# A mixture-of-experts token pass: gate logits with tokens on partitions, expert coefficients spread by a 0/1 product

## The chip, the cores and the metric

The kernel runs on one core of a Trainium2 chip (trn2). The metric is the device time of one execution in microseconds; lower is better. A core has TensorE (PE), VectorE (DVE), ScalarE (ACT), GpSimd (POOL) and SyncE (SP), which here starts all DMAs. The engines run side by side and wait for each other by semaphores.

## What is computed

The input x has 4 x 1024 tokens of 128 numbers. Three layers follow each other, each on the layer-normalised input: x + 0.5 ffn, x + attention (16 heads, ALiBi, rotary), x + 0.5 ffn. Both ffn layers use the same weights. Cut to what matters:

```python
scores = sigmoid(xf @ gate.T)                      # N x 8 experts
sfc = scores + corr_bias
# of 2 groups of 4 experts keep the one whose two best sfc sum higher
sel = top_k(where(mask, sfc, 0.0), 2)
top = scores[sel] / (scores[sel].sum(-1) + 1e-20)  # two coefficients per token
lat = xf @ fc1_w.T
routed = sum over the two experts e of top_e * (relu2(lat @ w1[e].T) @ w2[e].T) @ fc2_w.T
shared = relu2(xf @ up_w.T) @ down_w.T             # relu2(a) = max(a, 0) ** 2
return routed + shared
```

## The kernel before

The program is a prologue (weights are loaded, turned and folded), `token_pass` number 1 (ffn, then q, k and v of the attention), a bound for the softmax, the attention, and `token_pass` number 2 (output projection of the attention, then ffn). The change lies in the prologue and in `token_pass`, which is built twice.

**Chunks.** A pass goes over eight chunks of 512 tokens, four tiles of 128 (`in_chunks`: lead, body for each chunk, tail). Every engine has its own list of steps in `body`, written out by hand; an engine does its steps in that order, and this order sets what stands behind what. PE's body, for chunk c: in pass 2 the projection of the next chunk; hidden 0 to 3 (the shared experts' 512 hidden features), hidden 4, then spread 0 to 3 with hidden 5 to 7 (the 8 x 64 routed features) between them; `turn` of the next chunk's normalised input after spread 0 and `gate` of the next chunk after spread 2 (L682 to L689); `turn_gate` of the next chunk; `outputs`. In pass 1 the q, k and v products of the chunk before come between the first tile of `outputs` and the other three.

**Precision.** x_t, the turned input, is kept as two fp32r parts, high (copied by ACT, L719) and low (high subtracted from it by DVE, L953), and each weight matrix as w_hi and w_lo. A product of the two is three products (`times_weights`, L557). A plain fp32 product, as in `outputs`, shows as two matmuls in the trace; a transpose or an fp32r product as one.

**Gate.** `gate` (L586) multiplies w[:, 0:128], of whose columns 8 are the gate and 120 are zero, as stationary operand with the 512 tokens: the logits come out with experts on partitions. ACT copies the 128 x 512 result to `logit_t` (L725), PE turns it by four transposes (`turn_gate`, L591), and ACT takes exp of 8 columns in each tile (L731). DVE's `route` (L985 to L1045) makes the two coefficients per token from that: some 20 small operations, `coef` being the last (L1043).

**Coefficients.** The routed hidden features lie with features on partitions and tokens in the row, so each coefficient has to stand on 64 partitions. ACT's `widen` repeats each of the 8 coefficients 64 times in the row, [128 tokens, 4 tiles, 512] (L740), behind everything else in its body, so right in front of the next chunk's relu 0. `spread_coef` m then turns four 128 x 128 blocks of it into a PSUM bank (L608), and DVE's `scale` m multiplies the squared features by that (L1053). Two banks are used in turn.

**The other engines.** ACT: relu of each hidden block (L751), the square of the routed ones (L758). POOL: the squares of the shared ones (L843), rstd by a power (L835); in pass 2 the rstd of the next chunk stands in front of the squares. DVE, in pass 1: scale 0 to 3 with the second layer norm of the chunk before between them (L924) and `take_low` after scale 1; moments (L902); rotary products (L1075); `route` of the next chunk; centre; `rotary_q`; `residual` (L1061). In pass 2: `merge` (L944), moments, centre (L924), scale 0 to 3 with `take_low` after scale 1, `normalise_o` (L933, L934), `route`, `residual`. SP: in the prologue all loads one behind the other (`fold_loads`, `loads`, `table_loads`, x, rope), in the passes the loads and stores of a chunk.

**Prologue.** DVE waits for all of `table_loads` (L348) and then does, in order, the casts and copies of the tables, the parts of the slopes, and w_all, w_out and w_lo, which end the prologue.

## Time and profile before

| | before |
|---|---|
| device time, median of 3 runs | 1017.91 us (1016.92 to 1019.26) |
| profiled execution, its own time | 1016.92 us |
| its span in the profile | 1016.9 us |
| PE matmul busy | 866.5 us (85%) |
| DVE busy | 605.9 us (60%) |
| ACT busy | 699.4 us (69%) |
| POOL busy | 151.0 us (15%) |
| pass 1, first to last instruction, about | 27 to 282 us |
| pass 2, about | 827 to 1017 us |

The times in the profile are microseconds from the start of the span. L557 is line 557 of the kernel. PE is the matmuls, PEld the weight loads, which overlap them; matmuls are pipelined, so the time from one start to the next says what one costs, and its duration says when its result is there. A group "x4" is four instructions in a row, and its duration runs from the start of the first to the end of the last. In brackets stands how long the engine had been idle in front of the instruction, and what it waited for. In names like p_ps_g the number of the pass is left out.

### The profile page before, as it was taken

How to read it: one execution, taken by the hardware profiler on the slowest of the kernel's cores; microseconds unless marked ns; L12 is line 12 of the kernel's file. 1: busy time of each engine (PE TensorE's matmuls, PEld its weight loads, DVE VectorE, ACT ScalarE, POOL GpSimd, SP SyncE). 2: the span in 40 equal slices, each digit the busy share in tenths (PEclk: the TensorE clock that was granted, in tenths of full speed). 3: DMA queues.
4: the chain of work that ended last, by engine and by line, in shares of the span. 5: the costliest groups of instructions: out<-in, count | busy, mean ns of one | idle time of the engine just before them, and what ended most of it. 6: DMA issues, size and time to landing. Idle time of an engine off the chain costs nothing. (4 is left out here: it accounts for less than half of the span.)

```text
span 1016.9 us, 17952 instructions
## 1 busy us (share of the span) xinstructions
PE 866.5 (85%) x5629; PEld 432.3 (43%) x5629; DVE 605.9 (60%) x1620; ACT 699.4 (69%) x890; POOL 151.0 (15%) x136
## 2 busy tenths in 40 slices
PE   3498888788608999999999999999999947887888
PEld 2376666666502222222222222222222216776777
DVE  3469888888634454555445544555445437777673
ACT  1264343444417999999999999999999924555453
POOL 5224343334310000000000000000000001123211
PEclk9999999998758999999999999999999977999999
DMA  5112022211153322343223432344223021122100
GB/s 170 31 32 74 29 60 73 65 61 54 54 104 63 46 42 41 51 59 43 40 42 53 59 41 39 43 54 59 41 38 47 15 70 34 42 64 62 41 11 22
DMA packets 55095, 52.58 MB, mean 52 GB/s; under 512 B 7405, under 2 KB 42677, under 8 KB 54849
## 3 DMA queue, kind: packets, MB, share of 16 engines
q1 hardware_dynamic: 55052, 52.06, 26.2%
q8 instruction: 21, 0.34, 0.1%
q14 instruction: 22, 0.18, 0.1%
HBM read 36.15 MB, written 15.86 MB: 51 GB/s over the span
## 5 line engine op out<-in xcount | busy, mean ns | idle before, releaser
L1624 ACT ACTIVATE at_weights<-at_scores 128x1024 f32<-128x1024 f32 x512 | 495.4, 1022 | 31.2 <-DVE at_scores L1593 27.0
L1593 DVE SCALAR_TENSOR_TENSOR at_scores<-diag,at_now,at_scores 128x128 f32<-128x128 f32 x512 | 181.2, 354 | 234.8 <-PE at_scores L1530 217.8
L1530 PE MATMUL at_scores<-q_op,k_op 75*128 75x512 bf16 (+7 forms) x1408 | 273.0, 325 | 26.4 <-POOL at_start L1508 19.2
L1545 PE MATMUL at_acc<-at_weights,at_v_op 128*9 128x512 f32 x2048 | 267.5, 595 | 0.5 <-ACT at_weights L1624 0.5
L1530 PEld LDWEIGHTS at_scores<-q_op,k_op 75*128 75x128 bf16 (+1 forms) x1408 | 109.4, 98 | 312.4 <-issue 179.0
L623 PE MATMUL p_ps_o<-w_out,p_hid 128*128 128x128 f32 x1024 | 120.2, 278 | 0.4 <-DVE p_hid L1053 0.4
L557 PE MATMUL p_ps_h<-p_xn_t,w_hi 128*128 128x512 f32 x256 | 96.5, 461 | 27.1 <-ACT p_relu L751 26.5
L623 PEld LDWEIGHTS p_ps_o<-w_out,p_hid 128*128 128x128 f32 x1024 | 117.8, 194 | 0.6 <-DVE p_hid L1053 0.6
L751 ACT ACTIVATE p_relu<-p_ps_h 128x512 f32<-128x512 f32 x128 | 74.8, 591 | 35.3 <-PE p_ps_h L557 33.2
L713 ACT ACTIVATE p_coef_wide<-p_coef 128x512 f32<-128x512 f32 x64 | 35.0, 617 | 78.2 <-DVE p_coef L1043 78.2
L868 POOL MEMSET p_minus_half<- 128x4 f32 x2 | 0.2, 104 | 518.5 <-POOLq L1433 518.5
L843 POOL TENSOR_TENSOR p_hid<-p_relu 128x512 f32<-128x512 f32 x64 | 64.7, 1041 | 26.3 <-ACT p_relu L751 26.3
L557 PEld LDWEIGHTS p_ps_h<-p_xn_t,w_hi 128*128 128x128 f32 x256 | 46.2, 211 | 49.0 <-ACT p_relu L751 42.9
L1545 PEld LDWEIGHTS at_acc<-at_weights,at_v_op 128*9 128x9 f32 x2048 | 30.4, 88 | 79.5 <-issue 68.1
L557 PE MATMUL p_ps_h<-p_xn_t,w_lo 128*128 128x512 f32 x128 | 55.3, 432 | 0.0
L835 POOL TENSOR_TENSOR p_rstd<-p_veps,p_minus_half 128x4 f32<-128x4 f32 x24 | 24.3, 1012 | 190.6 <-DVE p_veps L917 190.6
L713 ACT ACTIVATE p_v_ext<-p_ps_q 128x128 f32<-128x128 f32 x32 | 6.3, 283 | 57.3 <-PE p_ps_q L651 57.3
L578 PE MATMUL p_ps_t<-ident,p_xn 128*128 128x128 f32 x64 | 10.9, 298 | 36.6 <-DVE p_xn L924 36.6
L758 ACT ACTIVATE p_squared<-p_relu 128x512 f32<-128x512 f32 x64 | 40.4, 632 | 2.0
L713 ACT ACTIVATE p_xn_t<-p_ps_t 128x512 fp32r<-128x512 f32 x24 | 14.2, 592 | 38.8 <-PE p_ps_t L578 35.4
L1053 DVE TENSOR_TENSOR p_hid<-p_squared,p_ps_q 128x512 f32<-128x512 f32 x32 | 21.9, 684 | 23.7 <-PE p_ps_q L608 22.4
L924 DVE TENSOR_SCALAR p_xn<-p_x,p_mean,p_rstd 128x128 f32<-128x128 f32 x32 | 28.9, 964 | 9.6 <-POOL p_rstd L835 9.6
(165 smaller groups left out, 808.0 us busy)
## 6 DMA issues: line engine op xcount, KB each, us to landing
q_op<-q_parts SPq DMA_DIRECT2D x144, 64.0 KB
k_op<-k_parts SPq DMA_DIRECT2D x144, 64.0 KB
q_parts<-p_parts SPq DMA_DIRECT2D x8, 384.0 KB, 2.6
k_parts<-p_parts SPq DMA_DIRECT2D x8, 384.0 KB, 3.3
v_scratch<-p_v_ext SPq DMA_DIRECT2D x32, 72.0 KB, 1.6
at_v_op<-v_scratch SPq DMA_DIRECT2D x16, 144.0 KB, 13.1
o_scratch<-at_o_out SPq DMA_DIRECT2D x64, 36.0 KB
x_ln<-in_L_attn_x_dram SPq DMA_DIRECT2D x8, 256.0 KB, 3.7
```

What stands on the lines that cost most here:

```text
L557: last = nc.tensor.matmul(out, w[:, col:col + P], x_t[:, part, :], start=(i == 0), stop=(i == 2))
L623: last = nc.tensor.matmul(ps_o[:, t, :], hid[:, m, t * P:(t + 1) * P], w_out[:, m, :], start=(m == 0), stop=(m == HT - 1))
L713: return nc.scalar.activation(dst, src, ACT.Copy)
L751: nc.scalar.activation(relu[:, m, :], ps_h[:, m % 2, :], ACT.Relu).then_inc(relu_ready, 1)
L758: nc.scalar.activation(squared[:, m, :], relu[:, ST + m, :], ACT.Square).then_inc(sq_act, 1)
L835: nc.gpsimd.tensor_tensor(rstd[:, which, :], veps[:, which, :], minus_half[:, :], ALU.pow).then_inc(rstd_ready[which], 1)
L843: nc.gpsimd.tensor_tensor(hid[:, m, :], relu[:, m, :], relu[:, m, :], ALU.mult).then_inc(sq_pool, 1)
L924: return v.tensor_scalar(dst[:, t, :], src[:, t, :], mean[:, which, t:t + 1], rstd[:, which, t:t + 1], ALU.subtract, ALU.mult)
L1530: last = nc.tensor.matmul(scores[:, u % SLOTS, lo:hi], k_op[par][0:rows, j, kt * P:(kt + 1) * P], q_op[par][0:rows, j, lo:hi], start=True, ...
L1545: last = nc.tensor.matmul(acc[32 * j:32 * j + VW, cols], v_op[par][:, kt, VW * j:VW * (j + 1)], weights[:, kt % PSTEPS, j, cols], start=(k ...
L1593: v.scalar_tensor_tensor(out=block_at, in0=diag[:, 0, :], scalar=now[:, par, j, 0:1], in1=block_at, op0=ALU.mult, op1=ALU.add).then_inc(di ...
L1624: nc.scalar.activation(weights[:, kt % PSTEPS, j, :], scores[:, u % SLOTS, :], ACT.Exp).then_inc(slots_free, 1)
```

## The change

The gate's product is turned round: x_t is the stationary operand (12 loads of 128 x 128: four tiles, three terms), the 8 gate columns of w_hi and w_lo are the moving one, and the logits come out with tokens on partitions, [128, 4 x 8], in one bank. `take_logits` and `turn_gate` go (4 transposes and one ACT copy), and with them `logit_t`. `widen` goes too (4 ACT operations).

DVE's `route` ends with three operations instead of one: the coefficients rounded to fp32r, the exact ones, and the difference of the two, so that `coef_parts` holds 16 columns a tile. PE turns them in `turn_coef` (four transposes of 128 x 16), between hidden 3 and hidden 4 of the same chunk, ACT copies the [16, 512] result to `coef_t` in `take_coef`, between relu 3 and relu 4. `spread_coef` is then one fp32r product: `spread_rows` (16 x 128 of a 0/1 matrix that says which expert a feature belongs to, high and low rows both) with coef_t, in place of four transposes. The prologue loads that 0/1 matrix (16 x 512, on SP's queue behind `headsum_f32`) and DVE copies it to fp32r. The first chunk's `turn_gate` and `widen` in the leads go as well.

```diff
@@ prologue
                 (headsum_f32[:, :], consts["headsum"]),
+                (spread_f32[:, :], consts["spread"]),
                 (bias_f32[br, :, :], consts["biasrows"]),
...
                 v.tensor_copy(headsum[:, :], headsum_f32[:, :])
+                v.tensor_copy(spread_rows[:, :], spread_f32[:, :])
@@ PE
                 if c.at_least >= 1:
-                    pe.wait_ge(gate_exp, c.n)
-                times_weights(ps_g[:, :], 0, xn_t[:, c.half]).then_inc(gate_made, 1)
-
-            def turn_gate(c):
-                pe.wait_ge(gate_copied, c.n + 1)
+                    pe.wait_ge(coef_copied, c.n)
+                x_t = xn_t[:, c.half]
                 for t in range(TILES):
-                    last = nc.tensor.transpose(ps_g[:, t * P:(t + 1) * P], logit_t[:, t * P:(t + 1) * P],
+                    for i, (part, w) in enumerate(((0, w_hi), (1, w_hi), (0, w_lo))):
+                        last = nc.tensor.matmul(ps_g[:, EXPERTS * t:EXPERTS * (t + 1)], x_t[:, part, t * P:(t + 1) * P],
+                                                w[:, 0:EXPERTS], start=(i == 0), stop=(i == 2))
+                last.then_inc(gate_made, 1)
+
+            def turn_coef(c):
+
+                pe.wait_ge(coef_ready, c.n + 1)
+                for t in range(TILES):
+                    last = nc.tensor.transpose(ps_g[0:2 * EXPERTS, t * P:(t + 1) * P], coef_parts[:, t, :].bitcast(F32),
                                                ident[:, :])
-                last.then_inc(gate_turned, 1)
+                last.then_inc(coef_turned, 1)
...
-                for t in range(TILES):
-                    last = nc.tensor.transpose(wide_bank[m % 2][:, t * P:(t + 1) * P],
-                                               coef_wide[:, t, m * P:(m + 1) * P], ident[:, :])
-                last.then_inc(spread, 1)
+                nc.tensor.matmul(wide_bank[m % 2], spread_rows[:, m * P:(m + 1) * P], coef_t[:, :],
+                                 start=True, stop=True).then_inc(spread, 1)
...
+                turn_coef(c)
                 hidden(c, ST)
-                pe.wait_ge(wide_ready, c.n + 1)
+                pe.wait_ge(coef_copied, c.n + 1)
...
-                if not end:
-                    turn_gate(c.next())
-
                 outputs(c, [0])
@@ ACT
-            def widen(c):
-
-                act.wait_ge(coef_ready, c.n + 1)
+            def take_coef(c):
+
+                act.wait_ge(coef_turned, c.n + 1)
                 if c.at_least >= 1:
                     act.wait_ge(spread, RT * c.n)
-                for t in range(TILES):
-                    last = copy(coef_wide[:, t, :].rearrange("p (e i) -> p e i", i=INTER),
-                                coef[:, t, :].unsqueeze(2).broadcast_to([P, EXPERTS, INTER]))
-                last.then_inc(wide_ready, 1)
+                copy(coef_t[:, :], ps_g[0:2 * EXPERTS, :]).then_inc(coef_copied, 1)
@@ DVE, end of route
-                v.tensor_tensor(coef[:, :, :], chosen[:, :, :],
-                                crec[:, :].unsqueeze(2).broadcast_to([P, TILES, EXPERTS]),
-                                ALU.mult).then_inc(coef_ready, 1)
+                each = crec[:, :].unsqueeze(2).broadcast_to([P, TILES, EXPERTS])
+                v.tensor_tensor(coef_parts[:, :, 0:EXPERTS], chosen[:, :, :], each, ALU.mult)
+                v.tensor_tensor(coef[:, :, :], chosen[:, :, :], each, ALU.mult).then_inc(route_step, 1)
+                dve.wait_ge(route_step, r + 16)
+                v.tensor_tensor(coef_parts[:, :, EXPERTS:2 * EXPERTS], coef[:, :, :], coef_parts[:, :, 0:EXPERTS],
+                                ALU.subtract).then_inc(coef_ready, 1)
```

## Rows read from the trace of the kernel before

**Rows 1.** Three stretches: busy PE, PEld, DVE, ACT, POOL (instructions); clock, DMA share, GB/s

```profile
65.00:240.00 175.00, 142.64 (x875) 113.92 (x874) 151.60 (x386) 78.11 (x161) 70.36 (x59) 0.97 0.20 59
857.00:998.00 141.00, 121.56 (x819) 102.95 (x818) 102.69 (x288) 68.53 (x123) 30.05 (x30) 0.98 0.14 40
898.00:901.00 3.00, 3.00 (x11) 2.30 (x10) 1.07 (x2) 1.67 (x3) 0.00 (x0) 0.50 0.02 5
```

**Rows 2.** Waits of DVE in pass 1, 65 to 240 us: total, times, longest

```profile
DVE p_turn_a L1075 <- PE p_ps_q L557: 9.3, 12, 1.7
DVE p_hid L1053 <- PE p_ps_q L608: 4.3, 6, 0.7
DVE p_hid L1053 <- ACT p_squared L758: 3.3, 1, 3.3
```

**Rows 3.** Timeline of one period of pass 2: start, duration, PE and DVE

```profile
875.72 0.66 PE L578 MATMUL p_ps_t<-ident,p_xn 128*128 128x128 f32 x4 [2.61 <-DVE p_xn L924]
...
877.65 0.69 DVE L1053 TENSOR_TENSOR p_hid<-p_squared,p_ps_q 128x512 f32<-128x512 f32 x1 [1.39 <-PE p_ps_q L608]
...
879.00 0.73 PE L557 MATMUL p_ps_g<-p_xn_t,w_hi 128*128 128x512 f32 x2 [0.35 <-DVE p_xn_t L953]
...
879.56 0.39 PE L557 MATMUL p_ps_g<-p_xn_t,w_lo 128*128 128x512 f32 x1
...
879.79 0.60 PE L608 MATMUL p_ps_q<-ident,p_coef_wide 128*128 128x128 f32 x4
...
881.14 7.31 PE L623 MATMUL p_ps_o<-w_out,p_hid 128*128 128x128 f32 x64
...
882.34 0.17 DVE L989 TENSOR_SCALAR p_en<-p_en 128x32 f32<-128x32 f32 x1
...
887.31 0.19 DVE L1043 TENSOR_TENSOR p_coef<-p_chosen,p_crec 128x32 f32<-128x32 f32 x1
...
888.28 1.06 PE L566 MATMUL p_ps_q<-proj_t,p_o_norm 128*128 128x128 f32 x8
...
888.48 0.69 DVE L1061 SCALAR_TENSOR_TENSOR p_res<-p_ps_o,p_x 128x512 f32<-128x512 f32 x1 [0.98 <-PE p_ps_o L623]
...
889.43 0.69 DVE L944 TENSOR_TENSOR p_x<-p_x_biased,p_ps_q 128x512 f32<-128x512 f32 x1 [0.26 <-PE p_ps_q L566]
...
897.15 0.66 PE L578 MATMUL p_ps_t<-ident,p_xn 128*128 128x128 f32 x4 [2.50 <-DVE p_xn L924]
...
903.62 1.61 PE L623 MATMUL p_ps_o<-w_out,p_hid 128*128 128x128 f32 x13
```

**Rows 4.** Timeline of v's product in pass 1: weight loads

```profile
170.19 0.30 PEld L651 LDWEIGHTS p_ps_q<-w_hi,p_xn_t 128*128 128x128 f32 x2 [0.52 <-DVE p_turn_a L1075]
...
170.41 0.19 PEld L651 LDWEIGHTS p_ps_q<-w_lo,p_xn_t 128*128 128x128 f32 x1
...
171.53 5.44 PEld L623 LDWEIGHTS p_ps_o<-w_out,p_hid 128*128 128x128 f32 x48
```

**Rows 5.** Timeline, waits in three other chunks (1 and 7; 0 of pass 2)

```profile
66.53 0.73 PE L557 MATMUL p_ps_h<-p_xn_t,w_hi 128*128 128x512 f32 x2 [0.85 <-ACT p_relu L751]
...
244.61 0.69 DVE L1053 TENSOR_TENSOR p_hid<-p_squared,p_ps_c 128x512 f32<-128x512 f32 x1 [0.65 <-ACT p_squared L758]
...
854.67 0.69 DVE L1053 TENSOR_TENSOR p_hid<-p_squared,p_ps_c 128x512 f32<-128x512 f32 x1 [0.75 <-ACT p_squared L758]
```

**Rows 6.** Timeline, first chunk of pass 1

```profile
42.86 0.19 DVE L1043 TENSOR_TENSOR p_coef<-p_chosen,p_crec 128x32 f32<-128x32 f32 x1
...
43.09 2.18 ACT L713 ACTIVATE p_coef_wide<-p_coef 128x512 f32<-128x512 f32 x4 [5.23 <-DVE p_coef L1043]
...
51.94 0.69 DVE L1053 TENSOR_TENSOR p_hid<-p_squared,p_ps_c 128x512 f32<-128x512 f32 x1 [8.88 <-PE p_ps_c L608]
```

**Rows 7.** Line 1021 in the whole span: duration in ns, least/median/most

```profile
L1021 DVE TENSOR_TENSOR p_above<-p_kept x16: 424/426/1365, 39.8 to 992.8; 128x256 f32<-128x256 f32 x16
```

**Rows 8.** Timeline of the prologue, DVE's wait for the tables

```profile
18.94 1.22 DVE L349 CAST bias_rows<-bias_f 30x2048 bf16<-30x2048 f32 x1 [6.22 <-DMA bias_sel<-const_biassel]
```

More of the change, by code:

```diff
@@ L64 @@
 UNITS = KT * GH
-ROUTE_STEPS = 15
+ROUTE_STEPS = 16
 QKV_COL = P
@@ L133, in shape_constants @@
     c["ident"] = np.eye(P, dtype=np.float32)
+    row, wide = np.arange(2 * EXPERTS)[:, None], np.arange(EXPERTS * INTER)[None, :]
+    c["spread"] = (row % EXPERTS == wide // INTER).astype(np.float32)
     c["headsum"] = (np.arange(P)[:, None] // HD == np.arange(HEADS)[None, :]).astype(np.float32)
@@ L442, in token_pass @@
         coef = sb("coef", [P, TILES, EXPERTS])
-        coef_wide = sb("coef_wide", [P, TILES, EXPERTS * INTER])
+        coef_parts = sb("coef_parts", [P, TILES, 2 * EXPERTS], F32R)
+        coef_t = sb("coef_t", [2 * EXPERTS, CHUNK], F32R)
         relu = sb("relu", [P, HT, CHUNK])
@@ L670, in lead @@
                 gate(Chunk(0, 0))
-                turn_gate(Chunk(0, 0))
             def body(c, end):
@@ L791, in body @@
                     relus(c, m)
+                take_coef(c)
                 for m in range(RT):
@@ L796, in body @@
                         take_xt(c.next())
-                if not end:
-                    take_logits(c.next())
                 if first and c.at_least >= 1:
@@ L805, in body @@
                     k_parts(c.next(-1))
-                if not end:
-                    widen(c.next())
             def lead():
                 take_xt(Chunk(0, 0))
-                take_logits(Chunk(0, 0))
                 exp_logits(Chunk(0, 0))
-                widen(Chunk(0, 0))
             def tail(c):
```

20 lines of the change are left out of this document (8 added, 12 removed).

## The prediction

> **What bounds the kernel now.** I read the busy shares by stage first. Attention fills the middle and isn't touched. The two token passes lie around it, and they are bound by different engines. In pass 1 DVE is busy 151.6 of 175 us and PE 142.6; in pass 2 PE is busy 121.6 of 141 us and DVE 102.7 [rows 1]. So a stretch of PE that gets shorter is worth little in pass 1, unless DVE waits for just that stretch.
>
> The table of waits says where DVE waits in pass 1: for the q/k products (9.3 us, a round trip that starts and ends on DVE and that the change leaves alone), and for the fourth spread, six times by 0.7 us [rows 2]. The rest of a chunk of about 29 us is DVE's own work, so what the change adds to DVE there is paid in full.
>
> The timeline gives pass 2. One period runs from the turn of the next chunk's input at 875.72 to the next such turn at 897.15, 21.43 us. PE works through from the turn over hidden 6 and 7, the spreads, the gate, turn_gate and outputs to project (done about 889.34); then DVE merges, takes moments and centres, and PE, which meanwhile does hidden 0 to 5 and spread 0, sits idle 2.50 us in front of the turn [rows 3]. Two kinds of PE time follow from that: what lies between turn and project is on the path, what lies between project and turn is covered by 2.5 us.
>
> **Price list.** Four 128-column transposes or products take their turn at 0.112 us each: 64 outputs span 7.31 us of which the last one's latency is 0.27 [rows 3], (7.31 - 0.27)/63 = 0.112. The row nearest to the new gate is v's product, which also has the fp32r x_t as stationary operand and three terms for each of four token tiles: its twelve weight loads begin at 170.19 and the next product's follow at 171.53, 1.34 us, again 0.112 each [rows 4]. A 512-column fp32r product lets its successor begin after 0.23 and is done after 0.40; the three of the gate need 0.79, 879.00 to 879.79 [rows 3].
>
> **1. Gate, twelve products with 8 moving columns instead of three with 512.** The trace has no product that moves so few columns, so the price is bounded. From above: a weight load of this form has a duration of 0.19 us by itself [rows 4]; if nothing of it overlaps, 12 x 0.19 = 2.3 us. From below: if the pace is set by the moving columns, 8 cost next to nothing and the load's issue sets it; taking half of the row's pace, 0.06, gives 0.7 us. I take the row itself, 0.112 and 1.34 us, since stationary operand, type and number of loads are the same and only the moving side shrinks: 0.55 us more than now.
>
> The Trainium skill, "TensorE: Matmul & The Clock Gate", says in the section on LDWEIGHTS that a load's time follows the count of its columns, about 107 ns for 128; twelve would be 1.28 us, an estimate by that page, and the row's 0.112 agrees. The same page's section "Back-to-back issue gap" gives products with up to 64 columns a gap of some 25 ns; by that alone the gate would take 0.3 us, and the sum would be some 15 us lower than mine. No row here shows such a gap.
>
> **2. No logit copy and no turn_gate.** Pass 2: gate begins at 879.00, outputs at 881.14, so 2.14 us, in which lie the gate, the fourth spread, a wait for ACT's copy and four transposes [rows 3]. After: 1.34 + 0.24 = 1.58. That is 0.56 earlier. exp follows directly behind the gate.
>
> **3. Spreads.** A spread of four transposes holds PE some 0.4 us and is done 0.60 after it begins; one product holds it 0.24 and is done after 0.40 [rows 3]. In pass 2 DVE's scale 1 waits for spread 1 (1.39 us of idle time), take_low stands behind it and the gate behind that [rows 3]; so the gate comes 0.2 earlier. Sum on the path from turn to project: 0.56 + 0.2 = 0.76. The fourth spread comes later than now, though: with the gate at 3.08 behind the turn, scale 3 ends near 5.6, while outputs, begun at 4.66, want it for their fifteenth product, at 6.2. No wait. Next late is DVE: behind scale 3 stand normalise and bias (0.6 us each, operations of the scale's size), route of 5.16 us (882.34 to 887.50) [rows 3] and the additions of point 4: done 12.24 behind the turn, residual until 12.93; project is then done at 12.95 instead of 13.7. DVE just keeps up. Seven periods (the last chunk has no next one): **-5.3 us**.
>
> **4. Route.** Two more operations on 32 elements a row. The row of the present one is 0.19 [rows 3]; two in a row follow each other after 0.1, one behind a wait after 0.22: 0.32 us. In pass 2 covered, as just shown. In pass 1 paid: DVE has no idle time between route and residual. There the longer gate counts too, since DVE already waits 0.7 us for the fourth spread behind it [rows 2]: 0.55 more, with 0.20 back because the single product is done sooner, so 0.35. Six chunks (1 to 6): 6 x (0.32 + 0.35) = **+4.0 us**.
>
> **5. coef turned (four transposes, 0.45 us of PE) and copied (ACT, 0.6 us: widen's four of the same length take 2.18 [rows 6]).** It stands between hidden 3 and 4. Queued behind its wait for coef are hidden 4 and all that follows on PE; behind take_coef on ACT, relu 4. In steady chunks coef is ready before, PE has the 2.5 us of cover and ACT is free there. In the last chunk of pass 2 nothing covers it: **+0.45**.
>
> **6. widen gone, 2.18 us of ACT per chunk, in front of relu 0.** In pass 1's steady chunks PE waits for that relu, but DVE doesn't come to the scale before its own work is done, so it costs nothing now and brings nothing. It shows where DVE waits for ACT. Chunk 1: PE idle 0.85 for relu 0 and DVE idle 3.3 for the square [rows 2, 5]; **-0.8**. Chunk 7: DVE idle 0.65 [rows 5]; **-0.6**. First chunk of pass 1: coef at 42.86, widen 43.09 to 45.27, then relu 0 and the hiddens 2 to 5 behind it, first scale at 51.94 [rows 6]. After, relus 0 to 3 run during the route. From coef to scale: turn 0.7 with its latency, copy 0.6, hidden 4 and 5, square: some 3.5 us instead of 9.1, a gain of 5.6. Against it: POOL's squares then run during the route. A DVE operation with two SBUF inputs that meets a POOL operation waits it out: L1021 is 0.43 as a rule and up to 1.37 [rows 7]. Four squares can cost up to 4 x 0.94 = 3.8; I take 2.6 of them: **-3.0** (between -1.8 and -5.5). The page "SBUF — State Buffer" of the Trainium skill calls the port pair of DVE and GpSimd an exclusive lock ("SBUF: two separate sides"), and the stretched L1021 agrees. First chunk of pass 2: the scale comes right behind centre with 0.75 of waiting [rows 5]; POOL's squares can't come earlier, being queued behind the next chunk's rstd. **-0.7**.
>
> **7. Prologue.** One more load of 32 KB on SP's queue in front of bias_f, bias_sel, x and rope, and one more DVE copy of 512 elements a row behind the wait for those tables, which is DVE's longest there (6.22 us) [rows 8]. 0.45 for the copy (up to 0.7), 0.35 for the load (0 to 0.5): **+0.8**.
>
> **Sum:** -5.3 + 4.0 + 0.45 - 0.8 - 0.6 - 3.0 - 0.7 + 0.8 = -5.15 us on the profiled execution's 1016.9. The median of the runs shown is 1.0 above it, so 1017.9 - 5.15 = **1012.8 us**.
>
> **Rivals.** (a) *Small products are cheap* (0.06 us each): each of 13 gates on the path (six in pass 1, seven in pass 2) is 0.64 shorter than I say, the two first ones, at the lower clock, some 0.7: 8.3 + 1.4 = 9.7, so 1003. For it: what moves is 8 columns. Against it: the rows with 128-column loads show 0.112 throughout, whatever the type. Chance 0.13. By the gap on the Trainium skill's page on TensorE, 0.025 us, the time would be near 998, an estimate.
>
> (b) *Slower: loads of the gate don't overlap.* Place: gate, between take_low and the fourth spread, in both passes. At 0.19 each it adds 12 x 0.078 = 0.94 to each of 15 gates: +14, so 1027. It decides from where 15 x 12 x d = 5.15, d = 0.029, a pace of 0.14 us. For it: so short a product hides nothing of the next load. Against it: v's loads begin 0.11 apart though each lasts 0.19 [rows 4]. Chance 0.15.
>
> (c) *The gains of the first chunks are lost and the clock falls more often.* A spell at the 1.2 GHz level (granted clock 0.50 between 898 and 901 [rows 1]) stretched the way from turn to outputs from 5.42 to 6.47 us [rows 3], by 1.05, after the 2.5 us of idle PE; in pass 2's first chunk PE will now be idle 4 us there, and twelve tiny products are thin work. With two or three more spells (+3) and the route of chunk 0 stretched in full (+1.2): 1016 to 1018, no change. Chance 0.17.
>
> **How the numbers follow.** Forecast 0.55, own range 1009 to 1017. The range of 1005 to 1020 leaves out most of (a) below and most of (b) above. The measurement tells 0.2%, 2 us, from no change. Faster: (a), and 0.53 of the forecast: 0.66. Within: 0.18. Slower: 0.16, nearly all (b).
>
> **What would show it.** Right: gate to fourth spread 1.3 to 1.4 us in both passes; pass 2's period near 20.7; pass 1's chunks 0.6 to 0.7 longer; DVE's wait for the spread in pass 1 near 1.05; PE no longer waiting for relu 0; the first scale of pass 1 near 50. Wrong: a gate under 0.8 us or over 1.7, route meeting POOL in the steady chunks, residual waiting for nothing in pass 2 while merge comes late, or more than three spells of the lower clock in pass 2's steady stretch.

## The result and the profile after

The changed kernel takes 1072.59 us (median of 4 runs, 1068.17 to 1074.65) against 1018.53 for the kernel before beside it (1016.92 to 1019.26): ratio 1.0529, 95% interval 1.0501 to 1.0556. It is slower by 5.3%; 1012.8 was forecast, in a range of 1005 to 1020. The profiled execution took 1074.45 us, its span is 1072.7. The changed kernel's line numbers: turn L585, gate L596, turn_coef L604, spread L620, outputs L634, project L573, scale L1050, residual L1058.

The same three stretches as in [rows 1], of the kernel after (the second one lies in pass 2's steady chunks, the third in one period of it):

```profile
65.00:240.00 175.00, 146.50 (x763) 111.93 (x763) 138.94 (x364) 62.20 (x125) 63.90 (x55) 0.88 0.19 57
866.00:1016.00 150.00, 134.10 (x636) 104.72 (x633) 90.17 (x250) 48.85 (x87) 30.05 (x30) 0.75 0.12 36
899.00:906.00 7.00, 6.46 (x18) 4.09 (x18) 3.06 (x5) 3.05 (x5) 0.40 (x1) 0.50 0.01 2
```

The column to read is the granted clock. It was 0.97 in pass 1 and 0.98 in pass 2 [rows 1] and is now 0.88 and 0.75, so PE spends half of pass 2 at the 1.2 GHz level. ACT has got less to do, as the change says (78 to 62 us in pass 1, in part because the slower pass gets through less work in the same stretch); DVE does less in the same stretch of time, because it waits.

DVE's waits in pass 1, 65 to 240 us, as in [rows 2]:

```profile
DVE p_hid L1050 <- PE p_ps_q L620: 13.7, 6, 2.8
DVE p_turn_a L1072 <- PE p_ps_q L564: 11.8, 10, 2.7
DVE p_hid L1050 <- PE p_ps_c L620: 3.2, 1, 3.2
```

The wait for the fourth spread, forecast at 1.05 a chunk, is 13.7/6 = 2.3.

One period of pass 2, PE (and the waits of DVE), as in [rows 3]:

```profile
896.82 0.50 PE L620 MATMUL p_ps_c<-p_coef_t,spread_rows 16*128 16x512 f32 x1
...
899.54 1.12 PE L585 MATMUL p_ps_t<-ident,p_xn 128*128 128x128 f32 x4 [2.22 <-DVE p_xn L918]
...
901.87 0.79 PE L620 MATMUL p_ps_q<-p_coef_t,spread_rows 16*128 16x512 f32 x1
...
902.59 1.22 PE L564 MATMUL p_ps_h<-p_xn_t,w_hi 128*128 128x512 f32 x2
902.79 0.69 DVE L1050 TENSOR_TENSOR p_hid<-p_squared,p_ps_q 128x512 f32<-128x512 f32 x1 [2.71 <-PE p_ps_q L620]
...
904.89 0.59 PE L596 MATMUL p_ps_g<-w_hi,p_xn_t 128*128 128x8 f32 x2
...
907.54 0.79 PE L620 MATMUL p_ps_q<-p_coef_t,spread_rows 16*128 16x512 f32 x1
...
908.26 9.36 PE L634 MATMUL p_ps_o<-w_out,p_hid 128*128 128x128 f32 x64
908.47 0.69 DVE L1050 TENSOR_TENSOR p_hid<-p_squared,p_ps_q 128x512 f32<-128x512 f32 x1 [2.68 <-PE p_ps_q L620]
...
917.46 1.06 PE L573 MATMUL p_ps_q<-proj_t,p_o_norm 128*128 128x128 f32 x8
...
926.32 0.90 PE L585 MATMUL p_ps_t<-ident,p_xn 128*128 128x128 f32 x3 [1.96 <-DVE p_xn L918]
```

Read as starts, beside the period before and, ahead of its time, one of experiment e11 in which the clock stayed up (us):

| stretch of a period | before | after | e11 |
|---|---|---|---|
| turn to gate | 3.28 | 5.35 | 3.04 |
| gate to fourth spread | 0.79 | 2.65 | 1.36 |
| fourth spread to outputs | 1.35 | 0.72 | 0.31 |
| outputs to project | 7.14 | 9.20 | 7.14 |
| turn to project together | 12.56 | 17.92 | 11.85 |
| project to next turn | 8.87 | 8.86 | 8.89 |

All of the loss lies between turn and project; the way from project to the next turn has moved by less than 0.03. PE still idles 2.0 to 2.2 us in front of the turn (2.50 before), but now the clock is down behind every one of pass 2's seven turns, and stays down through hidden 6 and 7, the gate, three spreads and a part of outputs. From turn to project the six such stretches that end in a project take 17.5 to 18.3 us, against 12.5 to 13.6 before.

The first chunk of pass 1 and the prologue, as in [rows 6] and [rows 8]:

```profile
19.09 1.22 DVE L355 CAST bias_rows<-bias_f 30x2048 bf16<-30x2048 f32 x1 [6.34 <-DMA bias_sel<-const_biassel]
...
20.41 0.41 DVE L357 CAST spread_rows<-spread_f 16x512 fp32r<-16x512 f32 x1
...
39.61 1.30 DVE L1015 TENSOR_TENSOR p_above<-p_kept 128x256 f32<-128x256 f32 x1
...
41.27 1.15 DVE L1018 TENSOR_TENSOR p_equal<-p_equal,earlier 128x256 f32<-128x256 f32 x1
...
42.45 1.15 DVE L1022 TENSOR_TENSOR p_above<-p_above,p_equal 128x256 f32<-128x256 f32 x1
...
49.74 0.69 DVE L1050 TENSOR_TENSOR p_hid<-p_squared,p_ps_c 128x512 f32<-128x512 f32 x1 [4.00 <-PE p_ps_c L620]
```

### The profile page after: what moved, and what is told of

Its sections match the earlier page's. It is cut to its first block and busy times, and to the rows that moved or that the text cites. A ratio compares the mean times of both kernels' runs of the same rounds, so it can differ in the third digit from the quotient of the medians.

```text
span 1072.7 us, 17822 instructions
## 1 busy us (share of the span) xinstructions
PE 932.1 (87%) x5581; PEld 472.2 (44%) x5581; DVE 615.3 (57%) x1653; ACT 666.6 (62%) x826; POOL 151.0 (14%) x136
## 5 line engine op out<-in xcount | busy, mean ns | idle before, releaser
L634 PE MATMUL p_ps_o<-w_out,p_hid 128*128 128x128 f32 x1024 | 145.7, 313 | 0.0
L634 PEld LDWEIGHTS p_ps_o<-w_out,p_hid 128*128 128x128 f32 x1024 | 142.7, 228 | 3.7 <-issue 3.7
L564 PE MATMUL p_ps_h<-p_xn_t,w_hi 128*128 128x512 f32 x256 | 100.3, 477 | 1.9 <-ACT p_coef_t L721 0.7
L837 POOL TENSOR_TENSOR p_hid<-p_relu 128x512 f32<-128x512 f32 x64 | 65.2, 1048 | 25.1 <-ACT p_relu L750 25.1
L1050 DVE TENSOR_TENSOR p_hid<-p_squared,p_ps_q 128x512 f32<-128x512 f32 x32 | 21.9, 684 | 54.0 <-PE p_ps_q L620 53.9
L585 PE MATMUL p_ps_t<-ident,p_xn 128*128 128x128 f32 x64 | 14.1, 360 | 38.9 <-DVE p_xn L918 38.9
L596 PE MATMUL p_ps_g<-w_hi,p_xn_t 128*128 128x8 f32 x128 | 33.8, 337 | 13.4 <-DVE p_xn_t L947 13.2
L596 PEld LDWEIGHTS p_ps_g<-w_hi,p_xn_t 128*128 128x128 f32 x128 | 31.3, 300 | 19.4 <-DVE p_xn_t L947 16.4
```

Source lines behind the costliest of these rows:

```text
L564: last = nc.tensor.matmul(out, w[:, col:col + P], x_t[:, part, :], start=(i == 0), stop=(i == 2))
L596: last = nc.tensor.matmul(ps_g[:, EXPERTS * t:EXPERTS * (t + 1)], x_t[:, part, t * P:(t + 1) * P], w[:, 0:EXPERTS], start=(i == 0), stop=( ...
L634: last = nc.tensor.matmul(ps_o[:, t, :], hid[:, m, t * P:(t + 1) * P], w_out[:, m, :], start=(m == 0), stop=(m == HT - 1))
L837: nc.gpsimd.tensor_tensor(hid[:, m, :], relu[:, m, :], relu[:, m, :], ALU.mult).then_inc(sq_pool, 1)
L1050: v.tensor_tensor(hid[:, ST + m, :], squared[:, m, :], wide_bank[m % 2], ALU.mult).then_inc(scaled_ready, 1)
```

## The experiments

Every kernel is cut at the same four places: the start of the last `residual` of pass 1, the first and the last one of pass 2 (seven periods between them), and the end of the span. The first column of parts runs from the start of the span. The last 3.4 us are the same in all but e2 (4.1). "Clock" is the granted clock over the seven periods. The parts are those of the profiled execution; the time is that of the one execution made, or the median of several. "Filler" is a row of products of 512 columns over 128 rows that nobody reads, put where PE waits. Up to e12 all but before and after were executed once, on several chips. The kernel before took between 1015.4 and 1022.1 us in 28 executions, so smaller differences between single executions are read by parts: the five executions whose pass 1 is that of the kernel before (before, e8, e13, e14, e16) take 197.3 to 199.0 us from pass 1's first residual to its last.

| kernel | time | pass 1 done | to first of pass 2 | seven periods | clock |
|---|---|---|---|---|---|
| before | 1018.5 | 263.3 | 603.8 | 146.4 | 0.98 |
| after | 1072.6 | 281.4 | 609.5 | 178.4 | 0.77 |
| e1 old gate | 1055.5 | 271.7 | 609.9 | 168.6 | 0.82 |
| e2 old spread | 1023.1 | 268.1 | 604.3 | 144.7 | 0.98 |
| e3 gate moves 128 columns | 1080.1 | 286.9 | 609.5 | 178.5 | 0.77 |
| e4 spread over 128 rows | 1037.2 | 275.3 | 604.9 | 151.8 | 0.90 |
| e5 e1 and e4 | 1033.3 | 272.3 | 606.7 | 149.1 | 0.93 |
| e6 32, 64, 96, 128 rows | 1043.1 | 274.3 | 609.4 | 154.1 | 0.89 |
| e7 after, filler in pass 2 | 1038.1 | 281.2 | 605.3 | 146.4 | 0.98 |
| e8 before, filler in pass 2 | 1017.1 | 262.1 | 605.4 | 144.4 | 1.00 |
| e9 after, norms later | 1080.0 | 287.1 | 609.1 | 178.5 | 0.77 |
| e10 e5, norms later | 1031.2 | 270.7 | 606.5 | 148.8 | 0.93 |
| e11 e4, filler, norms later | 1031.4 | 279.0 | 605.5 | 141.7 | 0.99 |
| e12 after, filler in both | 1030.0 | 268.1 | 608.3 | 148.4 | 0.97 |
| e13 only pass 2 changed | 1016.2 | 263.1 | 604.8 | 143.3 | 0.98 |
| e14 gate in pass 2, filler | 1014.0 | 261.4 | 604.8 | 142.7 | 1.00 |
| e15 e12 over 128 rows | 1023.1 | 271.5 | 605.6 | 142.1 | 0.99 |
| e16 e8 in more runs | 1016.5 | 262.9 | 605.1 | 144.4 | 1.00 |

By this table the 55.8 us between the two spans are 18.1 in pass 1, 5.7 up to pass 2's first residual, 31.9 in the seven periods and 0.1 behind them. Of the 5.7, 5.0 lie between the first chunk's turn and project (17.46 us instead of 12.45, behind 4.72 us of idle PE), and this stretch stands ahead of the table's seven periods: they hold the other six.

### Which part of the change: e1 to e4

e1 takes the gate back (three products of 512 columns, logit copy, turn_gate) and keeps the new spread:

```diff
-                for t in range(TILES):
-                    for i, (part, w) in enumerate(((0, w_hi), (1, w_hi), (0, w_lo))):
...
-                last.then_inc(gate_made, 1)
+                times_weights(ps_g[:, :], 0, xn_t[:, c.half]).then_inc(gate_made, 1)
+            def turn_gate(c):
...
+            def take_logits(c):
...
```

> The changed kernel with its old gate (three products of 512 columns, ACT's copy of the logits, four transposes) and the new spread. Theory G (the lower clock comes from the gate: for its time the array moves 8 columns per load): clock back to 0.95, pass 2's period near 21, time 1015 to 1022. Theory S (it comes from the spread: the 16-row product counts for little): stays near 1065 to 1075, clock 0.90. Theory B (neither alone, both thin PE's work in the same stretch): halfway, 1035 to 1055. Theory W (the waits that turn_coef and take_coef add are the loss, the clock only follows): near 1072, since these stay.

e2 is the other half, the kernel before with nothing but the new gate (exp reads the 32 columns directly):

```diff
-                times_weights(ps_g[:, :], 0, xn_t[:, c.half]).then_inc(gate_made, 1)
+                for t in range(TILES):
+                    for i, (part, w) in enumerate(((0, w_hi), (1, w_hi), (0, w_lo))):
+                        last = nc.tensor.matmul(ps_g[:, EXPERTS * t:EXPERTS * (t + 1)], x_t[:, part, t * P:(t + 1) * P],
+                                                w[:, 0:EXPERTS], start=(i == 0), stop=(i == 2))
```

> The kernel before with the new gate alone (12 loads, 8 columns), widen and the spread by transposes as before. Theory G: near 1060 to 1075, clock 0.90. Theory S: 1010 to 1020, clock 0.95. Theory B: 1035 to 1055. Theory W: 1010 to 1020, since turn_coef and take_coef are gone.

e3 is the changed kernel whose gate moves 128 columns instead of 8 (120 of them zeros):

```diff
-                        last = nc.tensor.matmul(ps_g[:, EXPERTS * t:EXPERTS * (t + 1)], x_t[:, part, t * P:(t + 1) * P],
-                                                w[:, 0:EXPERTS], start=(i == 0), stop=(i == 2))
+                        last = nc.tensor.matmul(ps_g[:, t * P:(t + 1) * P], x_t[:, part, t * P:(t + 1) * P],
+                                                w[:, 0:P], start=(i == 0), stop=(i == 2))
```

> The changed kernel, but each of the gate's twelve products moves all 128 columns w[:, 0:128] (120 of them zero) in place of 8; the number of loads stays. At the full clock the pace is set by the load, 0.112 us, with 8 and with 128 columns alike, so by itself this costs nothing. Theory G: 1010 to 1025, clock 0.95. Theory S and W: no change, 1068 to 1075. Theory B: in between.

e4 is the changed kernel whose spread runs over 128 rows, 112 of them zeros, in both operands (coef_t is set to zero once in each pass's lead, and the prologue's load of the 0/1 matrix gets eight times as long):

```diff
-        coef_t = sb("coef_t", [2 * EXPERTS, CHUNK], F32R)
+        coef_t = sb("coef_t", [P, CHUNK], F32R)
...
-        spread_rows = sb("spread_rows", [2 * EXPERTS, EXPERTS * INTER], F32R)
+        spread_rows = sb("spread_rows", [P, EXPERTS * INTER], F32R)
```

> The changed kernel, but the spread's operands have 128 rows, 112 of them zero, in place of 16; the same 512 columns. Theory S: 1010 to 1025, clock 0.95, and if it is the count of rows that keeps a spread at 0.42 us from start to start, that falls to 0.24. Theory G and W: no change, 1068 to 1075. Theory B: in between.

Measured: 1055.5, 1023.1, 1080.1 and 1037.2, beside 1021.7 for the kernel before on that chip. The number of columns that the gate moves is not the cause: e3's periods are those of after. The rows of the spread are most of it: zeros alone, which change nothing of what is computed and of what waits for what in the passes, take 35 us back. So Theory W falls, whose waits e4 leaves in place, and Theory G too: with the new gate alone (e2) pass 2 keeps its clock of 0.98. e1 gives 17 us back, at the edge of Theory B: the old gate helps beside the 16-row spreads, but the clock still fell behind six of pass 2's seven turns. In pass 1 the new gate alone does cost something: e2 needs 203.8 us from the first residual to the last, with a clock of 0.92 against 0.96.

The next rows show what a spread costs PE, with the clock up. In the kernel after, the next product starts 0.42 behind it:

```profile
128.30 0.40 PE L564 MATMUL p_ps_h<-p_xn_t,w_lo 128*128 128x512 f32 x1
128.63 0.49 PE L620 MATMUL p_ps_c<-p_coef_t,spread_rows 16*128 16x512 f32 x1
129.05 0.66 PE L585 MATMUL p_ps_t<-ident,p_xn 128*128 128x128 f32 x4
```

And it starts 0.33 behind the product ahead of it, not 0.23 as after a product of the same shape. In e11 (below), over 128 rows, both distances are 0.23 to 0.24:

```profile
935.56 0.40 PE L565 MATMUL p_ps_h<-p_xn_t,w_lo 128*128 128x512 f32 x1
935.80 0.39 PE L624 MATMUL p_ps_q<-p_coef_t,spread_rows 128*128 128x512 f32 x1
936.03 0.62 PE L565 MATMUL p_ps_h<-p_xn_t,w_hi 128*128 128x512 f32 x2
```

So a 16-row spread costs 0.33 + 0.42 - 0.23 = 0.52 us of PE's order, not 0.24: 1.1 us more a chunk, 18 us in 16 chunks if all of it were on the path. That price can't be the 5.4 us a period; the clock is the rest.

The price is not one of the 16-row product by itself. In the last chunk of pass 2 no gate stands between the last two spreads, and they follow each other (kernel after, PE, then the weight loads):

```profile
1060.81 0.40 PE L564 MATMUL p_ps_h<-p_xn_t,w_lo 128*128 128x512 f32 x1
1061.13 0.50 PE L620 MATMUL p_ps_c<-p_coef_t,spread_rows 16*128 16x512 f32 x1
1061.47 0.39 PE L620 MATMUL p_ps_q<-p_coef_t,spread_rows 16*128 16x512 f32 x1
1061.79 0.60 PE L634 MATMUL p_ps_o<-w_out,p_hid 128*128 128x128 f32 x3
```
```profile
1061.13 0.18 PEld L620 LDWEIGHTS p_ps_c<-p_coef_t,spread_rows 16*128 16x128 f32 x1 [0.36 <-issue]
1061.24 0.18 PEld L620 LDWEIGHTS p_ps_q<-p_coef_t,spread_rows 16*128 16x128 f32 x1
```

From the product ahead of the two spreads to the product behind them it is 0.98 to 0.99 us; with one spread between it is 0.75 (128.30 to 129.05). So the second 16-row product adds 0.24, as one of 128 rows does, and has the duration 0.39. What costs the 0.28 is the change from 128 rows to 16 and back: the first one's weight load begins together with its product, while the second one's begins 0.23 ahead of it and is hidden. The same distances stand in all six kernels here that have this pair of 16-row spreads (after, e1, e3, e7, e9, e12).

### The price by rows, and both parts back: e5, e6

e5 puts both edits together: old gate, and spread over 128 rows.

> The changed kernel with the old gate (three 512-column products, logit copy, turn_gate) and the spread's product over 128 rows of which 112 are zero. What is left of the change is turn_coef, take_coef, the two route operations, the missing widen and the prologue's load and copy. The spread over 128 rows alone came to 1037. Theory R1, the rest of the loss is the new gate (2.6 us instead of 1.3 at the lower clock, and thin work): 1020 to 1026, with spells of the lower clock in pass 2 as in the kernel before, two of 3.4 us in the steady stretch. Theory R2, the rest is the round trip of the coefficients (turn_coef's wait in front of hidden 4, take_coef in front of relu 4) and route's two operations: 1034 to 1038 as with the new gate, and the table of waits shows PE behind turn_coef in both kernels alike.

e6 gives the four spreads 32, 64, 96 and 128 rows:

```diff
+                rows = 32 * (m + 1)
-                nc.tensor.matmul(wide_bank[m % 2], spread_rows[:, m * P:(m + 1) * P], coef_t[:, :],
+                nc.tensor.matmul(wide_bank[m % 2], spread_rows[0:rows, m * P:(m + 1) * P], coef_t[0:rows, :],
```

> The changed kernel with the spread's products over 32, 64, 96 and 128 rows for m = 0, 1, 2 and 3 (zeros behind the 16 that matter). At full clock the 16-row product held PE 0.42 us and the 128-row one 0.24. Theory: the pace follows from the rows in one step, so 32 rows cost 0.42 as 16 do and 64 or 96 already 0.24. Rival: it falls gradually with the rows, 0.40, 0.34, 0.28, 0.24. Rival: rows have nothing to do with it and 0.42 was the wait for a cold engine: all four 0.24. Time: if each row taken away lets the clock fall more often, between 1037 and 1072, near 1045 to 1060; if only very few rows do, 1037 to 1040.

e6, timeline of PE in pass 1 and pass 2, at full clock:

```profile
67.73 0.50 PE L622 MATMUL p_ps_c<-p_coef_t,spread_rows 32*128 32x512 f32 x1
68.16 0.66 PE L586 MATMUL p_ps_t<-ident,p_xn 128*128 128x128 f32 x4
...
915.66 0.50 PE L622 MATMUL p_ps_q<-p_coef_t,spread_rows 64*128 64x512 f32 x1
916.09 0.73 PE L565 MATMUL p_ps_h<-p_xn_t,w_hi 128*128 128x512 f32 x2
...
916.90 0.40 PE L622 MATMUL p_ps_c<-p_coef_t,spread_rows 96*128 96x512 f32 x1
```

32 and 64 rows hold PE 0.43 between products of 128, as 16 do; 96 rows start 0.24 behind the product ahead of them and show the short duration of 128. It is a step, but between 64 and 96 rows, not where I had put it. The time, 1043.1, lies between the two that I had written down. The Trainium skill, "TensorE: Matmul & The Clock Gate", section "Why this matters for your kernels", has a single product over 32 rows take the same time as one over 128. The trace agrees for the second of two 16-row products in a row (0.24 more, duration 0.39), and not for one that stands between products of 128 rows, which costs 0.52 instead of 0.24; there the measurement decides.

e5 came to 1033.3, neither theory's. By parts the old gate is worth 5.5 us of pass 1 from its first residual (206.0 against 211.5 in e4) and 2.7 of the seven periods. 15 us of the loss remain though gate and rows are both back (the spread is still one product in place of four transposes). They lie in pass 1 (+9.0), in the lead of pass 2 (+2.9) and in its periods (+2.7). R2 named two possible places; e9 to e12 look into them.

### The idle time in front of the products: e7, e8

e7 fills PE's idle time in front of the turn in pass 2 with eight products whose result nobody reads; the rest of the changed kernel stays, 16-row spread and gate too:

```diff
             def turn(c):
-                pe.wait_ge(norm_ready, c.n + 1)
                 if c.at_least >= 1:
                     pe.wait_ge(xt_ready, c.n)
...
+                if not first and c.at_least >= 1:
+                    for _ in range(8):
+                        nc.tensor.matmul(ps_t[:, :], w_hi[:, 0:P], w_hi[:, 0:CHUNK], start=True, stop=True)
+                pe.wait_ge(norm_ready, c.n + 1)
```

> The changed kernel with eight products of 512 columns over 128 rows, whose result nobody reads, into turn's bank in front of the wait for the normalised input in pass 2. Theory F, the spells at 1.2 GHz start from PE's idle time in front of the turn and the thin work only prolongs them: the periods of pass 2 go from 27.1 us back to 21 to 22.5, the time is 1035 to 1045. Theory S, the 16-row products lower the clock by themselves, whatever PE did before them: the spells of 13.7 us per period stay, and the time is 1068 to 1080.

e8 does the same with six products in the kernel before.

> The kernel before with six such products (1.4 us at full clock, inside the 2.5 us of idle time) in front of the turn in pass 2. Theory F: the spells of 3.4 us in pass 2's steady stretch, about 1 us each, and part of the long ones at its start go away: 1016 to 1020 against 1021.7. Rival: the filler delays the turn as often as it keeps the clock: 1021 to 1026.

e7: the seven periods go from 178.4 to 146.4 us, by work that is added. A stretch of about one of its periods, and the seven periods of e7 and of after, from the view by stretches:

```profile
900.00:922.00 22.00, 21.61 (x133) 16.88 (x134) 16.58 (x47) 8.63 (x16) 5.01 (x5) 1.00 0.17 48
886.50:1032.90 146.40, 144.05 (x865) 113.15 (x863) 100.25 (x279) 58.23 (x103) 34.10 (x34) 0.98 0.14 40
```
```profile
890.90:1069.20 178.30, 164.92 (x816) 130.31 (x814) 100.34 (x279) 58.21 (x103) 34.08 (x34) 0.77 0.12 33
```

PE is busy 144 us instead of 165 although it runs 49 instructions more. Theory S in its strict form, that 16-row products lower the clock whatever stands beside them, falls; Theory F holds. e7 also gives the price of the clock alone: with the same 16-row spreads and the clock up, turn to project takes 12.36 us, and 17.5 to 18.3 in after. What e4 and e7 show together is that either remedy brings most of pass 2 back: full products in the idle time (all of it), or full rows in the spread (26.6 of 32 us). The clock fell behind every turn where an idle time of 2 us met the few-row spreads behind it; with the old gate (e1) it still did behind most of them, and with idle time or few rows gone it mostly stayed up. The Trainium skill, same page, section "A second HAM failure mode: psum-queue depth-cycling", says that frequent short idle times between groups of products can make the clock swing; the trace agrees only in part. In after PE's idle times in front of pass 2's seven turns sum to 17.1 us and the clock of the seven periods is 0.77, and with six of them filled (e7) it is 0.98; but the kernel before idles 15.2 us in front of six of its turns, at 0.98.

### The order on PE in pass 1: e9, e10

In pass 1, norms stands in front of turn_coef and makes PE idle for POOL's squares. Waits of PE in the kernel after, 65 to 240 us:

```profile
PE p_ps_q L672 <- POOL p_squares L855: 11.6, 5, 2.5
PE p_ps_g L596 <- DVE p_xn_t L947: 10.4, 6, 2.4
```

```diff
+                turn_coef(c)
+                hidden(c, ST)
                 if first and c.at_least >= 2:
                     norms(c.next(-2))
-                turn_coef(c)
-                hidden(c, ST)
```

> The changed kernel with norms moved behind hidden 4 in pass 1, so that turn_coef and hidden 4 no longer stand behind norms' wait for POOL's squares (11.6 us of idle PE time in the steady stretch of pass 1, 2.3 a chunk). Theory W, the order on PE costs pass 1 part of its 18 us: the idle time of PE is split, the spells at 1.2 GHz behind it get shorter, the chunks of pass 1 are 1 to 2 us shorter, time 1060 to 1067. Theory C, the clock falls from the thin products wherever they stand: nothing moves, 1069 to 1075.

> The kernel with the old gate and the spread over 128 rows (1033.3, of which pass 1 holds 9 us more than the kernel before and pass 2 2.7 more), with norms moved behind hidden 4 in the same way. Theory W: pass 1's chunks go from 30.2 to 31.2 back to 29.1 to 30, time 1025 to 1029. Theory C, what is left is route's two operations, the prologue and the lead: 1031 to 1035.

Neither moved as the order's theory wanted. e9 reads 5.5 us slower than the profiled execution of after, but 5.1 of it stand before its first residual (68.8 against 63.7), where the two kernels still do the same steps. The stretch of 44 to 64 us, e9 and then after:

```profile
44.00:64.00 20.00, 18.49 (x62) 13.95 (x63) 8.93 (x36) 6.29 (x11) 1.22 (x2) 0.50 0.00 1
```
```profile
44.00:64.00 20.00, 18.07 (x103) 15.04 (x104) 12.66 (x51) 5.96 (x11) 1.50 (x2) 0.83 0.00 1
```

So the same code met a clock of 0.50 once and of 0.83 once (e3 too had 0.50 there, and 68.8): one execution's clock can differ by 5 us in the first chunk alone. Counted from the first residual to pass 1's last, after has 217.7, e9 218.3, e3 218.1: norms' place is worth nothing. e10, from its first residual (65.2), has 205.5 against 206.0 in e5 (66.3). Theory W falls.

### How much is the clock altogether: e11, e12, e15

e11 is e4 with the filler in pass 2 and norms later.

> The changed kernel with its new gate, the spread over 128 rows, norms behind hidden 4, and eight unread products of 512 columns in front of the turn in pass 2. If the losses are the 16 rows, the idle time in front of the turn and the place of norms, and they add up: pass 2's seven periods 20.7 to 21.2 each (145 to 148 us instead of 151.8 with 128 rows alone), pass 1 some 4 us shorter, time 1022 to 1028. If they don't add up: 1030 to 1036. Below 1018 it would beat the kernel before; I don't expect that, since route's two operations and the longer gate stay in pass 1.

e12 is the changed kernel, 16 rows and all, with the filler of e7 and, in pass 1, six such products in front of norms and six in front of the gate, each behind the wait that frees their bank; of the edit, the place in front of the gate:

```diff
+                if first and c.at_least >= 1:
+                    for _ in range(6):
+                        nc.tensor.matmul(ps_g[:, :], w_hi[:, 0:P], w_hi[:, 0:CHUNK], start=True, stop=True)
                 pe.wait_ge(xt_ready, c.n + 1)
```

> The changed kernel, 16-row spread and all, with unread products of 512 columns wherever PE waits long: eight in front of the turn in pass 2, and in pass 1 six in front of norms and six in front of the gate (each 1.4 us at full clock in idle times of 2.0 to 2.5). If the clock is the loss and idle PE the trigger, pass 1 loses most of its spells at 1.2 GHz too: pass 1 from 18 us over the kernel before to 5 to 9 us over, time 1024 to 1030. If thin products lower the clock in pass 1 whatever stands beside them: 1036 to 1041.

e12 is at 1030.0, 42.6 us under the median of the kernel after, and issues 134 products of 512 columns more than that. Pass 1's stretch in e12, whose row in after has a clock of 0.88:

```profile
65.00:240.00 175.00, 158.77 (x907) 119.75 (x907) 148.91 (x386) 63.31 (x130) 67.86 (x58) 0.98 0.20 59
```

e11, timeline of one period of pass 2, the source of the third column above:

```profile
911.47 2.02 PE L586 MATMUL p_ps_t<-w_hi 128*128 128x512 f32 x8
913.87 0.66 PE L589 MATMUL p_ps_t<-ident,p_xn 128*128 128x128 f32 x4 [0.38 <-DVE p_xn L922]
...
916.91 0.39 PE L600 MATMUL p_ps_g<-w_hi,p_xn_t 128*128 128x8 f32 x2 [0.53 <-DVE p_xn_t L951]
917.15 0.25 PE L600 MATMUL p_ps_g<-w_lo,p_xn_t 128*128 128x8 f32 x1
...
918.27 0.47 PE L624 MATMUL p_ps_q<-p_coef_t,spread_rows 128*128 128x512 f32 x1
918.58 7.31 PE L638 MATMUL p_ps_o<-w_out,p_hid 128*128 128x128 f32 x64
925.72 1.06 PE L574 MATMUL p_ps_q<-proj_t,p_o_norm 128*128 128x128 f32 x8
```

With clock and rows kept, turn to project is 11.85 us, 0.71 under the kernel before (0.76 was forecast), and the seven periods are 141.7, 4.7 under it. (The forecast's 5.3 counts seven such stretches. Six lie in the seven periods, so 4.6 is the figure to compare.) In pass 1 e11 has no filler, and its chunks are as long as e4's or longer, at a clock of 0.87, so the whole is 1031.4: the three losses don't add up. e15 adds 128 rows to e12:

> The changed kernel in both passes, the spread over 128 rows, and unread products in all three places (turn in pass 2; norms and gate in pass 1). If the clock is all that went wrong, what is left is the sum that was forecast without the gain of the first chunks: pass 1 +4 to +5, pass 2 -4.7, prologue +1, lead +1 to +3: 1019 to 1024. If something else is left: 1026 to 1030 as with 16 rows and the same fillers (1030.0).

1023.1 in 11 runs, ratio 1.0049 (1.0032 to 1.0065). Its periods are 142.1; what is left is pass 1, 8.2 us over the kernel before.

### A version that beats both: e13, e14, e16

e13 has pass 1 as before and pass 2 changed, with 128 rows and the filler. e14 has pass 1 as before, in pass 2 the new gate alone (spread by transposes, as before) and six filler products. e16 is e8 in more runs. (Each of the first two builds pass 1 from the old function and pass 2 from the new one.)

> Pass 1 exactly as in the kernel before; pass 2 as changed, with the spread over 128 rows and eight unread products of 512 columns in front of the turn. Theory: the change's sum for pass 2 (5.3 us less over seven periods) holds once the clock is kept, and all that is left of the loss is in pass 1 and its first chunk. Pass 2's periods 20.6 to 21 against 21.3 to 22.6, 141.7 us against 146.4, prologue +1, lead of pass 2 +1 to +2: 1014 to 1017, against 1018.3. Rival: the lead of pass 2 and the prologue eat the gain: 1017.5 to 1020.

> Pass 1 exactly as before; pass 2 with the new gate alone (spread by transposes of the widened coefficients as before) and six unread products in front of the turn. The new gate alone had pass 2's seven periods at 144.7 with one spell. If gate and filler add: 142.5 to 144 for the seven, no prologue, no turn_coef: 1014 to 1017. Rival, the product spread is what makes e13's periods short: 144.4 as with the filler alone, 1016 to 1018.

> The kernel before with six unread products in front of the turn in pass 2 alone, one look at which gave 1017.1 against 1018.6. Expected 1016 to 1018, a ratio between 0.9975 and 1.000; it says how much of e13 and e14 is the filler.

| kernel | median, runs | ratio to before | 95% interval |
|---|---|---|---|
| e13 | 1016.17 (12) | 0.9967 | 0.9951 to 0.9982 |
| e14 | 1013.95 (6) | 0.9950 | 0.9931 to 0.9970 |
| e15 | 1023.10 (11) | 1.0049 | 1.0032 to 1.0065 |
| e16 | 1016.51 (12) | 0.9983 | 0.9970 to 0.9996 |

The kernel before had 1018.26 in 28 runs beside them. e13, e14 and e16 are faster than it by their intervals, though by little, and e14 is the fastest of all kernels here, by 0.5%. The filler gives 0.17% of that, the gate in pass 2 the larger rest (142.7 instead of 144.4 us in the seven periods, though the intervals of e14 and e16 touch). The product spread adds nothing in the end: e13 has it at its full 128 rows, and its periods and its time are no better than e14's. With the clock up its stretch from turn to project is shorter (11.85 to 11.88 us against 12.23 to 12.27), but the clock was down in a part of outputs in two of its periods (13.5 us each) and in none of e14's. e14's periods, from the view by stretches:

```profile
866.20:1008.90 142.70, 132.62 (x909) 113.33 (x907) 98.02 (x268) 67.96 (x124) 34.11 (x34) 1.00 0.15 41
```

## Why the prediction was wrong

**The step that failed is the clock.** The sum has no term for it: it took the clock of [rows 1], 0.97 and 0.98, as a given of the kernel, while the change itself lowered it. Rival (c) had the place right (behind PE's idle time in front of the turn, and 4 us of it in pass 2's first chunk, where 4.7 were measured) but priced it by two or three more spells of about 1 us. The clock fell behind every one of pass 2's seven turns, and the lower clock cost not 1.05 but 5.1 to 6.0 us each time (17.5 to 18.3 us from turn to project, against 12.36 in e7 with the same products and the clock up), because it stayed down into outputs. (c) also blamed the wrong products: with the twelve small ones alone (e2) pass 2 kept 0.98, and with the 16-row spreads alone (e1) it fell to 0.82. e7 and e12 show directly what the clock is worth: 34 and 43 us come back by doing more.

**Point 3, the spread**: sized by the row of a 128-row fp32r product, 0.24 and done after 0.40. Measured 0.42 and 0.49, and 0.10 more in front of it. The product's rows were in the diff (16), and no row of the trace of before had so few in an fp32r product; I took the price without a bound. The error is 0.28 a spread at full clock, and it comes from the changes between 128 and 16 rows, as the pair of spreads in the last chunk shows. The few-row spreads are also what, together with the idle time, let the clock fall (e4).

**Point 1, the gate**: right at full clock. Twelve products take 1.34 to 1.36 us (918.27 - 916.91 = 1.36 in e11), 0.112 each, neither 0.06 (a) nor 0.19 (b): both rivals fall. Nor does the gap of some 25 ns show here that the Trainium skill, "TensorE: Matmul & The Clock Gate", section "Back-to-back issue gap", gives for products of up to 64 columns; each product here has a load of its own. At the 1.2 GHz level the gate takes 2.65, which the forecast had no term for. **Point 2** held: turn to project 0.71 shorter in e11, where point 3's 128 rows were given too; with 16 rows and the clock up it is 0.2 (12.36 in e7 against 12.56).

**Point 4, route**: the additions are 0.33 a chunk (915.25 to 915.58, the three operations of the end), as forecast. The wait for the fourth spread is 2.3 in after and 8.7/6 = 1.45 in e12, where the clock is kept, against 1.05: of the 0.4 more, 0.19 is the spread's own (0.10 in front of it, 0.09 of duration); the rest wasn't traced. Chunks 1 to 7 of pass 1 take 203.8 us in e12 against 198.6 before, +5.2 where +2.6 was forecast.

**Point 5**: turn_coef is covered in pass 2, but take_coef makes PE wait 0.18 for it in four of the seven periods, in time that the idle time in front of the turn covers; the 0.45 of the last chunk didn't show (15.78 us from the residual before it to its own, against 15.79). **Point 6**: the first scale came at 49.74 against 51.94, 2.2 earlier, which is the forecast's 3.0 less the prologue's 0.8; route was stretched by POOL's squares three times, by 0.87, 0.73 and 0.72, 2.3 in all where 2.6 was taken. But of those 2.2 only 1.0 was left at the first residual (63.69 against 64.72), and nothing at the second (95.56, 95.60): chunk 1's forecast gain of 0.8 didn't come. The way to pass 2's first residual lost 5.7 instead of gaining 0.7, 5.0 of it by the lower clock behind the first turn. **Point 7**: the copy took 0.41 instead of 0.45, the wait 0.12 more instead of 0.35.

So at full clock the terms of the gate, the logits and the prologue were about right, the spread's and pass 1's wait and first chunks were not, and the sum was the forecast of another kernel, one whose clock holds.

**What stays open.** With fillers and full rows (e15) pass 1 takes 207.2 us from its first residual to its last, e12 with 16 rows takes 203.8, and the kernel before 198.6. That is more than the 1.7 us between the five executions of one and the same pass 1; e15's clock in pass 1 was 0.94 and e12's 0.97, and why it fell in e15 wasn't traced. Which property of the few-row spreads brings the clock down, their rows, the change of rows around them, or the longer time they hold PE, wasn't separated: in e6 all change together. Why pass 1 slows with the new gate alone (e2) is open too. The lead of pass 2 is not: of the 4.5 us that it loses in e12, 4.3 lie from the first chunk's turn to project (16.77 us instead of 12.45), where PE idled 2.70 us in front of the turn and the clock fell; in e5 1.7 of 2.9.

## What to carry to other kernels

When a change makes PE's work smaller or thinner beside an idle time that is there already, count the clock as a term of its own: every stretch behind the idle time can come out at the 1.2 GHz level, and here that was some eight times the forecast's whole sum (42.6 of the 54.1 us came back in e12). Check it in the profile by the granted clock of each stage before any wait is read, since every wait for PE grows with it. Before a product is priced by a row of the trace, look for one with the same number of rows and the same neighbours, not only the same type and columns. Placing few-row products side by side would, by the pair in the last chunk, save 0.28 us for each further one; no run here tries it. Where PE waits anyway, unread full-size products in the gap are a cheap test of whether the clock is the cause, and sometimes a remedy.

## What the runs showed of the hardware

- An fp32r product with 512 columns over 16, 32 or 64 rows that stands between products of 128 rows is followed after 0.42 to 0.43 us at full clock and starts 0.33 behind the product ahead of it, 0.52 of PE's order in all; over 128 rows it is 0.24. Over 96 rows it starts 0.24 behind the product ahead. Zeros in the added rows are enough.
- The 0.28 more belong to the change of rows: the second of two 16-row products in a row adds 0.24, its weight load hidden, in six kernels alike.
- Twelve fp32r products of 8 columns, each with its own load of 128 x 128, take 0.112 us each at full clock (e11) and 0.21 at the lower one (904.89 to 907.54 in after, 2.65 with the change to the spread).
- In pass 2 of the changed kernel the clock was down behind every one of the seven turns, in front of which PE idled 2.0 to 4.7 us; eight unread products in it, or 128 rows in the four spreads, brought the granted clock of the seven periods from 0.77 to 0.98 or 0.90.
- The same code in the same place of two executions had a granted clock of 0.50 and of 0.83 (44 to 64 us), worth 5 us.
